# A state-space stage in one block: drive in PSUM, C rows by DMA, two products before two scans

## The chip, the cores and the metric

The kernel runs on one core of one Trainium2 chip. The metric is the device time of one execution in microseconds, lower is better. The core has five engines that run side by side and meet only at semaphores: TensorE (PE; its matmuls write into PSUM), VectorE (DVE), ScalarE (ACT), GpSimd (POOL) and SyncE (SP), which here issues most DMAs.

## The reference

Two decoder layers over 1024 tokens of 128 features, in float32. Layer 0 begins with a Mamba block, then attention to a context of 6404 rows (16 heads, one key and value head), then a mixture of experts; layer 1 has self-attention, attention to the context, and a mixture of experts. After each branch comes a residual sum and a layer norm. The change is in the Mamba block alone, cut here to what matters (256 inner features, 16 states, rank 8):

```
xi, z   = split(x @ W_in.T)                    # 256 features each
xc      = silu(causal_conv4(xi))
dt_r, B, C = split(xc @ W_xproj.T)             # 8, 16 and 16 columns
delta   = softplus(dt_r @ W_dt.T + b_dt)
for each state n of 16, each feature f of 256, along t:
    h[t] = exp(delta[t, f] * A[f, n]) * h[t-1] + delta[t, f] * xc[t, f] * B[t, n]
    y[t, f] += h[t] * C[t, n]
out     = ((y + D * xc) * silu(z)) @ W_out.T
x       = layernorm(x + out)
```

The kernel also makes, in the same stage, the keys and values of layer 0's context attention from the 6404 context rows, since PE and DVE are free for them there. A key is kept as a high half and a low half (float32r).

## The kernel before, in words

Features lie on the partitions (two halves `s` of 128), time (1024) along the free dimension. Each engine's program is written out by hand; its order of instructions is its order of work, and semaphores join the engines.

*Front* (first block, lines 464 to 613). PE makes `xz` (line 517), then value chunks (`keys.values`, line 351: 51 chunks of 128 context rows, each a float32 matmul of 8 columns in two passes), key ranges (`keys.keys`, line 341: 13 ranges of 512 columns), `dbc` (dt_r, B and C, line 531) and the step sizes (line 540: 8 rows contracted). ScalarE or DVE writes a range's high half (lines 362, 371), DVE its low half (line 380). DVE makes the convolution, copies `dbc` from PSUM (line 598), splits it in three bfloat16 parts (`split`, lines 399 to 403), and SyncE moves their B and C rows into `bc_rows` (line 488), whose tile GpSimd has filled with zeros (line 510). Six 1024-wide DVE instructions make `delta` and `u` = delta * xc (lines 611 to 613).

*States* (second block, lines 615 to 733, loops over the 16 states `n`). All tiles are 128 x 1024 and there is one of each:

- PE spreads row B[n] over 128 partitions into `b_all` (PSUM; `spread`, line 624, bfloat16 with 128 rows contracted), and C[n] into `c_ps`. One `b_all` serves both halves.
- ScalarE makes `decay` (line 649) and copies C to SBUF (line 654).
- DVE makes the drive, `drive[s] = b_all * u[s]`, for both halves, PSUM times SBUF into SBUF (line 661), then the two scans `state[s]` = scan(decay[s], drive[s]), both from SBUF (line 667).
- GpSimd makes the read product `read[s] = state[s] * C`, both from SBUF (line 676).
- PE adds `read[s]` to `y[s]` in PSUM with an identity matmul (`add_read`, line 640; four passes of 512 columns for one half).

The order on PE is: y addition of half 0 of state n-1, B of n+1, y addition of half 1, C of n+1. A scan of state n may overwrite `state[s]` when GpSimd has read it, and a read product may overwrite `read[s]` when PE has added it.

*Tail.* DVE gates (y * silu(z), line 723), PE makes the output (line 703), and `residual_norm` (line 142) follows in a block of its own; its first instruction is line 166. After it the context attention begins.

Of the kernel before, what the change touches and what calls it, by code (L numbers as in the profile page):

```python
# [16 lines left out]
F32 = mybir.dt.float32  # L17
# [124 lines left out]
def residual_norm(k, tag, branch, added=False, store=None):  # L142
# [5 lines left out]
    with ExitStack() as tmp:  # L148
# [6 lines left out]
        turned = k.ps(tag + "_turned", [P, T], tmp)  # L155
# [128 lines left out]
class ContextKeys:  # L284

    CUT = 26
    RANGES = [(c0, min(HALF, CTX - c0)) for c0 in range(0, CTX, HALF)]

    def __init__(self, k, banks):
        self.k = k
        self.banks = banks
        self.v_ps = banks[:, HALF:HALF + NCH * HD].rearrange("p (c e) -> p c e", e=HD)
# [3 lines left out]
        self.v_ready = k.sem("ctx_v_ready")  # L298
# [5 lines left out]
    def bank(self, r):  # L304

        b = (4, 5, 6, 7, 0, 4, 5, 6, 7, 2, 3, 0, 2)[r]
        return self.banks[0:SPAN2, b * HALF:(b + 1) * HALF]

    def replicate(self, pool, w_kv):
# [10 lines left out]
        ins.then_inc(self.rep_ready, 1)  # L320
        pool.wait_ge(k.q_w_loaded, 16)
# [7 lines left out]
    def keys(self, pe, ranges, after=None):  # L329

        nc, k = self.k.nc, self.k
        for r in ranges:
            c0, n = self.RANGES[r]
            if r == 0:
                pe.wait_ge(self.ctx_loaded[0], 16)
                pe.wait_ge(self.rep_ready, 1)
            if c0 <= self.CUT * P < c0 + n:
                pe.wait_ge(self.ctx_loaded[1], 16)
            if r >= 5:
                pe.wait_ge(self.k_done, {5: 1, 6: 2, 7: 3, 8: 4, 9: 5, 10: 5, 11: 5, 12: 10}[r])  # L340
            nc.tensor.matmul(self.bank(r)[:, 0:n], k.wk_rep[:], k.ctx_T[:, c0:c0 + n], start=True,
                             stop=True).then_inc(self.k_made, 1)
# [13 lines left out]
    def high_on_act(self, act, ranges):  # L356

        nc, k = self.k.nc, self.k
        for r in ranges:
            c0, n = self.RANGES[r]  # L360
            act.wait_ge(self.k_made, r + 1)
            nc.scalar.activation(k.key_stack[:, c0:c0 + n], self.bank(r)[:, 0:n], ACT.Identity,
                                 bias=k.shift_one[0:SPAN2, :]).then_inc(self.k_high, 1)

    def high_on_dve(self, dve, ranges):

        nc, k = self.k.nc, self.k
        for r in ranges:
            c0, n = self.RANGES[r]
            dve.wait_ge(self.k_made, r + 1)  # L370
            nc.vector.tensor_scalar(k.key_stack[:, c0:c0 + n], self.bank(r)[:, 0:n], k.shift_one[0:SPAN2, :], None,
                                    ALU.add).then_inc(self.k_high, 1)

    def halves(self, dve, ranges):

        nc, k = self.k.nc, self.k
        for r in ranges:
            c0, n = self.RANGES[r]
            dve.wait_ge(self.k_high, r + 1)
            nc.vector.scalar_tensor_tensor(out=k.key_stack[:, c0:c0 + n], in0=k.key_stack[:, c0:c0 + n].bitcast(F32),  # L380
                                           scalar=k.half_sel[0:SPAN2, :], in1=self.bank(r)[:, 0:n], op0=ALU.mult,
                                           op1=ALU.add).then_inc(self.k_done, 1)
# [7 lines left out]
    def take_values(self, dve):  # L390
# [3 lines left out]
        nc.vector.tensor_copy(k.val_ones[0:TAIL, full, 0:HD], self.v_ps[0:TAIL, full, :])  # L394
# [11 lines left out]
def mamba(k):  # L406
# [4 lines left out]
    LOADS = 6  # L411
    ctx = ExitStack()
    with ctx:
# [13 lines left out]
        conv = k.key1_T[:, 2 * T:4 * T].rearrange("p (s t) -> p s t", s=2)  # L427
        xc = k.sb("xc", [P, 2, T], F32, ctx)
        delta = k.sb("delta", [P, 2, T], F32, ctx)
        u = k.sb("u", [P, 2, T], F32, ctx)  # L430
        dbc = k.key1_T[0:ROWS, CTX - T:]

        bc_rows = k.sb("bc_rows", [P, NS, T], BF16, ctx)
        pick = k.sb("bc_pick", [P, 2, P], BF16, ctx)
        early = k.val1[:].rearrange("p c e -> p (c e)")
        decay = early[:, 0:2 * T].rearrange("p (s t) -> p s t", s=2)
        c_all = early[:, 2 * T:4 * T].rearrange("p (s t) -> p s t", s=2)
        state = early[:, 4 * T:6 * T].rearrange("p (s t) -> p s t", s=2)
        dbc_part = [state[0:ROWS, i // 2, (i % 2) * HALF:(i % 2 + 1) * HALF].bitcast(BF16) for i in range(3)]
        dbc_rest = [decay[0:ROWS, i, :] for i in range(2)]  # L440

        read = xpad[:, :, 0:T]
        soft = drive = conv
# [6 lines left out]
        dbc_split, dlt_ready, log_ready = k.sem("dbc_split"), k.sem("dlt_ready"), k.sem("log_ready")  # L450
        act_step, a_exp = k.sem("mamba_act_step"), k.sem("a_exp")
        rows_moved, pick_set, rows_zeroed = k.sem("rows_moved"), k.sem("pick_set"), k.sem("bc_rows_zeroed")
        b_ready, c_ready, b_used, c_copied = k.sem("b_ready"), k.sem("c_ready"), k.sem("b_used"), k.sem("c_copied")
        decay_ready, read_ready, y_added = k.sem("decay_ready"), k.sem("read_ready"), k.sem("y_added")
        scanned = k.sem("scanned")
        gated, out_ready = k.sem("y_gated"), k.sem("mamba_out_ready")


        with ExitStack() as front:
# [1806 lines left out]
```

## Time and profile before

| | us |
|---|---|
| median of 3 runs | 2270.96 (2268.21 to 2271.05) |
| the profiled execution's own time | 2268.48 |
| its span, first to last instruction | 2266.8 |
| granted PE clock, mean over the span | 0.957 of full speed |
| PE busy | 2078.7 (92% of the span) |
| DVE busy | 1625.9 (72%) |
| ACT busy | 1332.4 (59%) |
| POOL busy | 163.8 (7%) |

The busy times are sums over the whole span, and stages with different limits stand in them side by side: the state-space stage is its first tenth, and GpSimd works nearly only there. A granted clock of 1.00 is 2.4 GHz, 0.50 is 1.2 GHz; a value between them for a stretch is a mean of the two. In a timeline row the first number is the start, the second the time that the instruction (or a merged run of them, x2 and more) took; the bracket is the idle time of the engine before it and what ended it. Line numbers are those of the kernel before. A name such as `sb_key_T` or `sb_val` may stand for another tile that lies in the same memory (drive and zs in `key1_T`, decay, C and state in `val1`).

### The profile page before, as it was taken

How to read it: one execution, taken by the hardware profiler on the slowest of the kernel's cores; microseconds unless marked ns; L12 is line 12 of the kernel's file. 1: busy time of each engine (PE TensorE's matmuls, PEld its weight loads, DVE VectorE, ACT ScalarE, POOL GpSimd, SP SyncE). 2: the span in 40 equal slices, each digit the busy share in tenths (PEclk: the TensorE clock that was granted, in tenths of full speed). 3: DMA queues.
4: the chain of work that ended last, by engine and by line, in shares of the span. 5: the costliest groups of instructions: out<-in, count | busy, mean ns of one | idle time of the engine just before them, and what ended most of it. 6: DMA issues, size and time to landing. Idle time of an engine off the chain costs nothing. (4 is left out here: it accounts for less than half of the span.)

```text
span 2266.8 us, 38983 instructions
## 1 busy us (share of the span) xinstructions
PE 2078.7 (92%) x15239; PEld 983.5 (43%) x15240; DVE 1625.9 (72%) x2162; ACT 1332.4 (59%) x2203; POOL 163.8 (7%) x161
## 2 busy tenths in 40 slices
PE   8666899999999999999999999899589997999988
PEld 4222353333333333333333333477433333777755
DVE  6997878988889888898888983223778883444345
ACT  4332247777777777777777778623247773333421
POOL 3574000000000000000000000000200010000000
PEclk8898899999999999999999999899879998999989
DMA  3000000000000000000000000011000000000011
GB/s 107 0 0 1 0 1 1 1 1 1 1 1 1 1 1 1 1 1 1 1 1 1 1 1 1 10 33 37 1 1 1 0 0 1 1 1 0 1 33 32
DMA packets 20767, 16.16 MB, mean 7 GB/s; under 512 B 5520, under 2 KB 20016, under 8 KB 20368
## 3 DMA queue, kind: packets, MB, share of 16 engines
q1 hardware_dynamic: 19440, 12.05, 1.9%
q8 instruction: 103, 1.69, 0.3%
q10 hardware_dynamic: 1184, 2.10, 0.2%
q14 instruction: 40, 0.33, 0.0%
HBM read 13.42 MB, written 0.52 MB: 6 GB/s over the span
## 5 line engine op out<-in xcount | busy, mean ns | idle before, releaser
L966 DVE TENSOR_REDUCE sb_max_partial<-ps_max_ps 128x1 f32<-128x1024 f32 (+1 forms) x896 | 958.1, 1107 | 99.2 <-PE ps_max_ps L809 93.6
L957 ACT ACTIVATE sb_probs<-ps_score_ps 128x512 f32<-128x512 f32 (+1 forms) x1632 | 885.5, 595 | 238.3 <-PE ps_score_ps L929 193.8
L809 PE MATMUL ps_max_ps<-sb_key_stack,sb_q_stack 64*128 64x512 f32 (+1 forms) x1664 | 602.0, 438 | 22.6 <-DVE sb_max_partial L966 10.3
L929 PE MATMUL ps_score_ps<-sb_q_stack,sb_key_stack 64*128 64x512 f32 x1632 | 592.1, 442 | 1.9 <-issue 0.4
L910 PE MATMUL ps_acc_ps<-sb_probs,sb_val_ones 128*32 128x256 f32 x6528 | 521.4, 391 | 0.8 <-ACT sb_probs L957 0.4
L929 PEld LDWEIGHTS ps_score_ps<-sb_q_stack,sb_key_stack 64*128 64x128 f32 x1632 | 241.1, 185 | 280.9 <-ACT sb_probs L957 266.3
L809 PEld LDWEIGHTS ps_max_ps<-sb_key_stack,sb_q_stack 64*128 64x128 f32 x1664 | 252.2, 185 | 152.9 <-DVE sb_max_partial L966 128.4
L910 PEld LDWEIGHTS ps_acc_ps<-sb_probs,sb_val_ones 128*32 128x32 f32 x6528 | 128.4, 108 | 293.6 <-ACT sb_probs L957 218.2
L1661 DVE TENSOR_REDUCE sb_s_max_partial<-ps_s_max_ps 128x1 f32<-128x512 f32 x256 | 170.2, 691 | 42.2 <-PE ps_s_max_ps L1586 35.2
L1651 ACT ACTIVATE sb_s_probs<-ps_s_score_ps 128x1024 f32<-128x1024 f32 x128 | 131.0, 1024 | 49.1 <-PE ps_s_score_ps L1623 46.7
L640 PE MATMUL ps_y<-sb_xpad,sb_ident 128*128 128x512 f32 x128 | 75.5, 721 | 51.6 <-POOL sb_xpad L676 51.6
L1878 DVE TENSOR_SCALAR_CACHE_REDUCE sb_x_scores<-ps_x_score_ps 128x1024 f32<-128x1024 f32 (+1 forms) x56 | 62.1, 1111 | 83.2 <-PE ps_x_score_ps L1819 83.2
L1819 PE MATMUL ps_x_score_ps<-sb_key_T,sb_x_q_buf 128*128 128x512 f32 (+1 forms) x208 | 102.1, 594 | 8.8 <-DVE sb_x_q_buf L1887 8.8
L1846 PE MATMUL ps_x_acc_ps<-sb_val,sb_x_turned 128*128 128x128 f32 (+1 forms) x816 | 109.1, 277 | 1.2 <-DVE sb_x_turned L1858 0.9
L1586 PE MATMUL ps_s_max_ps<-sb_s_k_stack_T,sb_s_q_stack_T 128*128 (+1 forms) x256 | 104.0, 408 | 6.3 <-PEq L1439 2.8
L676 POOL TENSOR_TENSOR sb_xpad<-sb_val 128x1024 f32<-128x1024 f32 x32 | 103.7, 3260 | 64.9 <-DVE sb_val L667 64.9
L1858 ACT COPY sb_x_turned<-ps_x_turn_ps 128x512 f32<-128x512 f32 (+1 forms) x52 | 29.6, 569 | 132.0 <-PE ps_x_turn_ps L1834 132.0
L667 DVE TENSOR_TENSOR_SCAN sb_val<-sb_val,sb_key_T 128x1024 f32<-128x1024 f32 x32 | 102.0, 3227 | 0.6
L1442 POOL MEMSET sb_s_mask<- 128x128 f32 x1 | 0.2, 204 | 1397.8 <-POOLq L160 1397.8
L1846 PEld LDWEIGHTS ps_x_acc_ps<-sb_val,sb_x_turned 128*128 128x128 f32 (+1 forms) x816 | 99.5, 191 | 3.5 <-issue 1.0
L1236 DVE SCALAR_TENSOR_TENSOR sb_e_acc<-ps_e_out_ps,sb_e_gates,sb_e_acc 128x128 f32<-128x128 f32 x136 | 36.7, 344 | 79.7 <-PE ps_e_out_ps L1216 79.7
L649 ACT ACTIVATE sb_val<-sb_delta,sb_a_neg 128x1024 f32<-128x1024 f32 x32 | 36.6, 1148 | 80.8 <-DVE sb_val L667 80.8
(285 smaller groups left out, 1791.8 us busy)
## 6 DMA issues: line engine op xcount, KB each, us to landing
sb_e_w<-L_ffn_rW SPq DMA_DIRECT2D x30, 128.0 KB, 2.1
sb_e_w<-L_ffn_W_T SPq DMA_DIRECT2D x24, 128.0 KB, 2.1
sb_ctx_T<-ctx_T SPq DMA_DIRECT2D x1, 1664.0 KB, 8.1
sb_ctx_T<-ctx_T ACTq DMA_DIRECT2D x1, 1538.0 KB, 9.4
sb_x_T<-x_T SPq DMA_DIRECT2D x1, 512.0 KB, 3.7
sb_x_tok<-x ACTq DMA_DIRECT2D x1, 512.0 KB, 11.6
sb_e_w<-L_ffn_sW SPq DMA_DIRECT2D x4, 128.0 KB, 2.2
out<-sb_x_tok SPq DMA_DIRECT2D x2, 256.0 KB, 2.4
```

Of the source, the lines that this page charges most:

```text
L667: nc.vector.tensor_tensor_scan(state[:, s, :], decay[:, s, :], drive[:, s, :], 0.0, ALU.mult, ALU.add).then_inc(scanned, 1)
L676: nc.gpsimd.tensor_tensor(read[:, s, :], state[:, s, :], c_all[:, parity, :], ALU.mult).then_inc(read_ready, 1)
L809: ins = nc.tensor.matmul(max_ps[:, u % 2, a:a + n], q_stack[rows(blk), blk // 2, h * P:(h + 1) * P], k.key_stack[rows(blk), c0 + a:c0 + a ...
L910: ins = nc.tensor.matmul(acc_ps[32 * q:32 * q + 32, 0:QUART], k.val_ones[:, v, :], probs[:, v % 3, q * QUART:(q + 1) * QUART], start=(v == ...
L929: nc.tensor.matmul(score_ps[:, e % 3, :], k.key_stack[rows(blk), c * P:(c + 1) * P], q_stack[rows(blk), blk // 2, j * HALF:(j + 1) * HALF] ...
L957: nc.scalar.activation(probs[0:n, c % 3, j * HALF:(j + 1) * HALF], score_ps[0:n, e % 3, :], ACT.Exp).then_inc(exp_done, 1)
L966: nc.vector.tensor_reduce(partial[:, h, r:r + 1], max_ps[:, u % 2, 0:RANGES[r][1]], AX.X, ALU.max).then_inc(unit_used, 1)
L1586: nc.tensor.matmul(max_ps[:, u % 2, :].rearrange("p (t c) -> p t c", t=4), block_of(q_T, h, u // 2), half_of(k_T, h, u % 2), start=True, s ...
L1651: nc.scalar.activation(probs[:, c % 2, :], score_ps[:, c % 2, :], ACT.Exp).then_inc(exp_done, 1)
L1661: nc.vector.tensor_reduce(partial[:, u // 2, u % 2:u % 2 + 1], max_ps[:, u % 2, :], AX.X, ALU.max).then_inc(unit_used, 1)
L1819: ins = nc.tensor.matmul(score_ps[:, local % 2, (g % 2) * HALF:(g % 2) * HALF + n], q_buf[:, s, :], k.key1_T[:, g * HALF:g * HALF + n], st ...
L1846: ins = nc.tensor.matmul(acc_ps[:, s, 0:D], turned[0:keys, local % 2, j * P:(j + 1) * P], k.val1[0:keys, c0 + j, :], start=(c0 + j == 0), ...
```

## The change

All in the state-space stage:

- One block instead of two, and unrolled loops instead of loops with a register. PSUM is one tile of eight banks from start to end.
- B and `dbc`: two float32r halves instead of three bfloat16 parts. ScalarE copies the high half, DVE subtracts. Four DMAs bring the B rows to two partitions for each of two groups of states; there is no tile of zeros. A spread is now two float32r matmuls that contract 2 rows, into `drive[s]`: each half has its own spread, and B[n+1] of half s waits for the scan of half s of state n.
- C: stored to DRAM once, and each state's row is loaded by SyncE, replicated over the 128 partitions, with three buffers. The C matmul and ScalarE's copy are gone.
- DVE multiplies the drive in place in PSUM, both halves first, then scans both; the scan reads decay from SBUF and drive from PSUM.
- PE's order per state and half: B of the next state, then the y addition.
- The last read product (state 15, half 1) is DVE's instead of GpSimd's.
- Key ranges 8 to 12 are made after the last state instead of before the first, and the value chunks 12 to 50 in one go ahead of the first state. The step-size matmuls of the two halves have key range 5 and 6 between and behind them.
- The gate writes to `read`, and the norm's transposes use the banks of y.

```diff
+                for i, made in ((0, dbc_high), (1, dbc_low)):
+                    sp.wait_ge(made, 1)
+                    for g in range(GROUPS):
+                        first = DR + g * SLOTS
+                        sp.dma_start(b_rows[32 * g + i:32 * g + i + 1, :, :].bitcast(F32), dbc_half[i][first:first + SLOTS, :].bitcast(F32)).then_inc(b_moved, 16)
...
+        def spread(pe, n, s):
+
+            lo = 32 * (n // SLOTS)
+            if n > 0:
+                pe.wait_ge(scanned, 2 * (n - 1) + s + 1)
+            for h in range(2):
+                ins = nc.tensor.matmul(half(drive[s], h), ones[lo:lo + 2, :], b_rows[lo:lo + 2, n % SLOTS, h * HALF:(h + 1) * HALF],
+                                       start=True, stop=True)
+            ins.then_inc(b_ready, 1)
...
+        def load_c(sp, n):
+
+            if n >= DEPTH:
+                sp.wait_ge(read_ready, 2 * (n - DEPTH) + 2)
+            sp.dma_start(c_all[:, n % DEPTH, :], c_dram[n:n + 1, :].to_broadcast([P, T])).then_inc(c_loaded[n % DEPTH], 16)
...
+            def _(pool):
...
+                for n in range(NS):
+                    c_is_loaded(pool, n)
+                    for s in range(2):
+                        if n == NS - 1 and s == 1:
+                            break
+                        pool.wait_ge(scanned, 2 * n + s + 1)
+                        if n > 0:
+                            pool.wait_ge(y_added, 2 * (n - 1) + s + 1)
+                        nc.gpsimd.tensor_tensor(read[:, s, :], state[:, s, :], c_all[:, n % DEPTH, :], ALU.mult).then_inc(read_ready, 1)
...
+            def _(pe):
...
+                keys.make(pe, 4)
+                pe.wait_ge(keys.k_done, 4)
+                pe.wait_ge(dbc_copied, 1)
+                for s in range(2):
+                    for h in range(2):
+                        ins = nc.tensor.matmul(half(xz[2 + s], h), w_dt[:, s * P:(s + 1) * P], dbc[0:DR, h * HALF:(h + 1) * HALF],
+                                               start=True, stop=True)
+                    ins.then_inc(dlt_ready, 1)
+                    if s == 0:
+                        pe.wait_ge(dbc_low, 1)
+                    keys.make(pe, 5 + s)
+                keys.make(pe, 7)
+                keys.values(pe, w_kv, range(12, NCH))
+
+                pe.wait_ge(keys.rep_ready, 2)
+                pe.wait_ge(b_moved, 16 * 2 * GROUPS)
+                pe.wait_ge(keys.v_taken, 1)
+                pe.wait_ge(keys.k_done, keys.LATE)
+                spread(pe, 0, 0)
+                spread(pe, 0, 1)
...
+                for n in range(NS):
                     for s in range(2):
+                        if n + 1 < NS:
+                            spread(pe, n + 1, s)
+                        elif s == 0:
+                            pe.wait_ge(scanned, 2 * n + 1)
+                            for r in range(keys.LATE, keys.LATE + 2):
+                                keys.make(pe, r)
+                        add_read(pe, n, s)
+                        if n == NS - 1 and s == 0:
+                            keys.make(pe, keys.LATE + 2)
+                for r in range(keys.LATE + 3, len(keys.RANGES)):
+                    keys.make(pe, r)
...
+                for n in range(NS):
                     for s in range(2):
+                        if n == 0:
+                            dve.wait_ge(log_ready, s + 1)
+                            dve.wait_ge(keys.k_done, keys.LATE)
+                            nc.vector.tensor_tensor(delta[:, s, :], delta[:, s, :], soft[:, s, :], ALU.add).then_inc(delta_ready, 1)
+                            dve.wait_ge(delta_ready, s + 1)
+                            link(nc.vector.tensor_tensor(u[:, s, :], delta[:, s, :], xc[:, s, :], ALU.mult))
+                        dve.wait_ge(b_ready, 2 * n + s + 1)
+                        nc.vector.tensor_tensor(drive[s], drive[s], u[:, s, :], ALU.mult).then_inc(driven, 1)
                     for s in range(2):
+                        dve.wait_ge(driven, 2 * n + s + 1)
+                        dve.wait_ge(decay_ready, 2 * n + s + 1)
+                        if n > 0:
+                            dve.wait_ge(read_ready, 2 * (n - 1) + s + 1)
+                        nc.vector.tensor_tensor_scan(state[:, s, :], decay[:, s, :], drive[s], 0.0, ALU.mult, ALU.add).then_inc(scanned, 1)
+                dve.wait_ge(scanned, 2 * NS)
+                c_is_loaded(dve, NS - 1)
+                dve.wait_ge(y_added, 2 * (NS - 1))
+                nc.vector.tensor_tensor(read[:, 1, :], state[:, 1, :], c_all[:, (NS - 1) % DEPTH, :], ALU.mult).then_inc(last_read, 1)
+                for r in range(keys.LATE, keys.LATE + 3):
+                    keys.halve(dve, r)
                 for s in range(2):
+                    dve.wait_ge(y_added, 2 * NS - 1 + s)
+                    nc.vector.tensor_tensor(read[:, s, :], y[s], zs[:, s, :], ALU.mult).then_inc(gated, 1)
+                for r in range(keys.LATE + 3, len(keys.RANGES)):
+                    keys.halve(dve, r)
```

## Rows read from the trace of the kernel before

**Rows 1.** The page: busy tenths of PE in 40 slices of the span
```profile
PE   8666899999999999999999999899589997999988
```

**Rows 2.** Timeline of the state loop: start us, duration us, engine, line, operation
```profile
68.47 4.18 POOL L676 TENSOR_TENSOR sb_xpad<-sb_val 128x1024 f32<-128x1024 f32 x1 [30.23 <-DVE sb_val L667]
71.62 1.22 DVE L661 TENSOR_TENSOR sb_key_T<-ps_b_all,sb_u 128x1024 f32<-128x1024 f32 x1
72.62 2.34 POOL L676 TENSOR_TENSOR sb_xpad<-sb_val 128x1024 f32<-128x1024 f32 x1
72.78 4.33 DVE L667 TENSOR_TENSOR_SCAN sb_val<-sb_val,sb_key_T 128x1024 f32<-128x1024 f32 x1
77.24 4.21 POOL L676 TENSOR_TENSOR sb_xpad<-sb_val 128x1024 f32<-128x1024 f32 x1 [2.29 <-DVE sb_val L667]
86.07 4.17 POOL L676 TENSOR_TENSOR sb_xpad<-sb_val 128x1024 f32<-128x1024 f32 x1 [2.32 <-DVE sb_val L667]
```

**Rows 3.** Three lines of the loop: ns min/median/max, first to last start
```profile
L661 DVE TENSOR_TENSOR sb_key_T<-ps_b_all,sb_u x32: 1191/1206/1225, 63.8 to 194.6; 128x1024 f32<-128x1024 f32 x32
L667 DVE TENSOR_TENSOR_SCAN sb_val<-sb_val,sb_key_T x32: 2257/2274/4328, 66.0 to 200.1; 128x1024 f32<-128x1024 f32 x32
L676 POOL TENSOR_TENSOR sb_xpad<-sb_val x32: 2335/3254/4205, 68.5 to 204.5; 128x1024 f32<-128x1024 f32 x32
```

**Rows 4.** Timeline of the front
```profile
10.55 1.01 ACT L555 COPY sb_xpad<-ps_front_ps 128x1024 f32<-128x1024 f32 x1 [1.44 <-PE ps_front_ps L517]
25.93 1.22 DVE L598 COPY sb_key_T<-ps_front_ps 40x1024 f32<-40x1024 f32 x1 [0.45 <-PE ps_front_ps L531]
27.77 4.11 DVE L380 SCALAR_TENSOR_TENSOR sb_key_stack<-sb_key_stack,sb_half_sel,ps_front_ps 128x512 fp32r<-128x512 f32 x5 [0.63 <-ACT sb_key_stack L362]
30.21 3.19 PE L351 MATMUL ps_front_ps<-sb_w_kv,sb_ctx_T 128*128 128x8 f32 x28
31.80 6.97 DVE L399 CAST sb_val<-sb_key_T 40x1024 bf16<-40x1024 f32 x1
54.36 0.57 DVE L393 COPY sb_val_ones<-ps_front_ps 128x400 f32<-128x400 f32 x1
61.18 1.22 DVE L613 TENSOR_TENSOR sb_u<-sb_delta,sb_xc 128x1024 f32<-128x1024 f32 x1
```

**Rows 5.** Stretches of the front: busy us by engine, granted clock, DMA
```profile
30.00:33.30 3.30, 3.30 (x29) 3.08 (x27) 3.08 (x4) 2.44 (x4) 3.30 (x1) 1.00 0.02 5
36.00:39.50 3.50, 3.50 (x5) 1.00 (x3) 3.47 (x2) 1.11 (x1) 2.23 (x1) 0.50 0.00 0
48.70:52.20 3.50, 3.50 (x19) 3.43 (x19) 0.00 (x0) 0.00 (x0) 0.00 (x0) 0.50 0.00 0
```

**Rows 6.** Timeline of PE in the state loop
```profile
63.51 1.06 PE L624 MATMUL ps_c_all<-sb_bc_rows,sb_bc_pick 128*128 128x512 bf16 x2
90.29 1.98 PE L640 MATMUL ps_y<-sb_xpad,sb_ident 128*128 128x512 f32 x4 [2.53 <-POOL sb_xpad L676]
92.11 0.59 PE L624 MATMUL ps_b_all<-sb_bc_rows,sb_bc_pick 128*128 x2
99.08 3.61 PE L640 MATMUL ps_y<-sb_xpad,sb_ident 128*128 128x512 f32 x4 [4.06 <-POOL sb_xpad L676]
```

**Rows 7.** Stretches of 8.79 us, one a state: first and last of 14
```profile
77.09:85.88 8.79, 4.72 (x10) 1.74 (x9) 8.75 (x6) 3.19 (x3) 6.50 (x2) 0.81 0.00 0
...
191.36:200.15 8.79, 5.87 (x14) 1.93 (x12) 8.75 (x6) 3.19 (x3) 6.48 (x2) 1.00 0.00 1
```

**Rows 8.** Timeline of the tail
```profile
204.55 5.40 PE L640 MATMUL ps_y<-sb_xpad,sb_ident 128*128 128x512 f32 x8 [4.48 <-POOL sb_xpad L676]
211.27 3.84 PE L703 MATMUL ps_b_all<-sb_w_out_T,sb_val 128*128 128x128 f32 x32 [1.32 <-DVE sb_val L723]
215.43 1.42 DVE L166 TENSOR_TENSOR sb_norm_res<-ps_b_all,sb_x_tok 128x512 f32<-128x512 f32 x2 [4.22 <-PEq L678]
```

**Rows 9.** The page: a DMA, its size, us from issue to landing
```profile
sb_x_tok<-x ACTq DMA_DIRECT2D x1, 512.0 KB, 11.6
```

More of the change, by code:

```diff
@@ L327, in replicate, with make @@
                                         float(HD) ** -0.5, None, ALU.mult)
-    def keys(self, pe, ranges, after=None):
+    def make(self, pe, r):
         nc, k = self.k.nc, self.k
[L332 to L342, printed above, removed]
+        c0, n = self.RANGES[r]
+        if r == 0:
+            pe.wait_ge(self.ctx_loaded[0], 16)
+            pe.wait_ge(self.rep_ready, 1)
+        if c0 <= self.CUT * P < c0 + n:
+            pe.wait_ge(self.ctx_loaded[1], 16)
+        if r in self.AFTER:
+            pe.wait_ge(self.k_done, self.AFTER[r])
+        nc.tensor.matmul(self.bank(r), k.wk_rep[:], k.ctx_T[:, c0:c0 + n], start=True, stop=True).then_inc(self.k_made, 1)
     def values(self, pe, w_kv, chunks):
@@ L354, in values, with high_on_act, high_on_dve, halve @@
             ins.then_inc(self.v_ready, 1)
[L356 to L382, printed above, removed]
+    def high_on_act(self, act, r):
+        act.wait_ge(self.k_made, r + 1)
+        self.k.nc.scalar.activation(self.columns(r), self.bank(r), ACT.Identity, bias=self.k.shift_one[:]).then_inc(self.k_high, 1)
+    def high_on_dve(self, dve, r):
+        dve.wait_ge(self.k_made, r + 1)
+        self.k.nc.vector.tensor_scalar(self.columns(r), self.bank(r), self.k.shift_one[:], None, ALU.add).then_inc(self.k_high, 1)
+    def halve(self, dve, r):
+        dve.wait_ge(self.k_high, r + 1)
+        self.k.nc.vector.scalar_tensor_tensor(out=self.columns(r), in0=self.columns(r).bitcast(F32), scalar=self.k.half_sel[:],
+                                              in1=self.bank(r), op0=ALU.mult, op1=ALU.add).then_inc(self.k_done, 1)
     def prepare(self, dve, link):
@@ L427, in mamba @@
         conv = k.key1_T[:, 2 * T:4 * T].rearrange("p (s t) -> p s t", s=2)
+        dbc = k.key1_T[0:ROWS, 4 * T:5 * T]
         xc = k.sb("xc", [P, 2, T], F32, ctx)
@@ L732, in mamba, with wide, half @@
-        residual_norm(k, "norm0", out_ps)
+        banks = k.ps("mamba_ps", [P, 8, HALF], ctx)
+        keys = ContextKeys(k, banks)
+        def wide(b):
+            return banks[:, b:b + 2, :].rearrange("p b t -> p (b t)")
+        xz = [wide(2 * c) for c in range(4)]
+        drive = [wide(0), wide(2)]
+        y = [wide(4), wide(6)]
+        out_ps = wide(2).rearrange("p (t e) -> p t e", t=NT)
+        def half(x, h):
+            return x[:, h * HALF:(h + 1) * HALF]
+        def spread(pe, n, s):
[6 more added lines that the diff above has]
+            ins.then_inc(b_ready, 1)
@@ new lines, in add_read @@
+        def add_read(pe, n, s):
+            if n == NS - 1 and s == 1:
+                pe.wait_ge(last_read, 1)
+            else:
+                pe.wait_ge(read_ready, 2 * n + s + 1)
+            for h in range(2):
+                ins = nc.tensor.matmul(half(y[s], h), k.ident[:], read[:, s, h * HALF:(h + 1) * HALF], start=False, stop=True,
+                                       skip_group_check=True)
+            ins.then_inc(y_added, 1)
+        def load_c(sp, n):
+            if n >= DEPTH:
+                sp.wait_ge(read_ready, 2 * (n - DEPTH) + 2)
+            sp.dma_start(c_all[:, n % DEPTH, :], c_dram[n:n + 1, :].to_broadcast([P, T])).then_inc(c_loaded[n % DEPTH], 16)
@@ L735, in stack_queries @@
+        residual_norm(k, "norm0", out_ps, turned=wide(4))
 def stack_queries(nc, link, whole, part, rest, stack, parts):
```

425 lines of the change are left out of this document (169 added, 256 removed).

## The prediction, before the changed kernel ran

> **What bounds the kernel now.** I read the page's slices first [rows 1]: the change lies in the first tenth of the span (slices 1 to 4), and the rest, where the TensorE (PE) is busy nine tenths of each slice, is the same code. So only the time from the start to the first instruction of `norm0`, which is at 215.43 us [rows 8], can move. It has three pieces: the front, up to the first scan at 66.0 [rows 3]; fifteen steps from one state's first scan to the next one's; and a tail.
>
> Then the durations by line and the single instructions of the state loop, VectorE (DVE) beside GpSimd (POOL). The 32 scans take 2257 to 4328 ns, the 32 read products 2335 to 4205 [rows 3]: each has two lengths. The scan takes 2.27 us, or 4.33 when a read product is under way at its start (72.78); the read product takes 2.34 (72.62), or 4.18 when it is issued just behind a scan (68.47) [rows 2]. They take turns: one state is two scans and two reads at about 2.2 each, and their sum is the distance of two states, 8.8 us (77.24 to 86.07, GpSimd's starts [rows 2]); from the second scan that starts at 77.11 to the one at 200.1 [rows 3] they are fourteen times 8.79. The drive product isn't in that sum: at 71.62 it runs inside the time in which read and scan take turns and takes its 1.22 us, and over all 32 its durations are 1191 to 1225 ns [rows 3]. It reads one operand from PSUM and one from SBUF; the scan reads two from SBUF. PE does not bound the loop: its y additions, even at half clock, end before anybody needs them.
>
> Fifteen steps are 131.85 us, and the last state's first scan ends where its second starts, at 200.1 [rows 3]; from there to `norm0` are 15.3 us.
>
> **The front.** Up to the copy of `dbc` at 25.93 [rows 4] nothing on the path changes. Before, what follows on the path is the three-part split, whose first cast took 6.97 us for 40 rows (a plain copy of the same size took 1.22) beside a GpSimd fill, late key ranges, and the last of six 1024-wide DVE instructions, at 61.18 to 62.4 [rows 4]. The change drops cast, fill and five of thirteen key ranges (they go to the tail). What is left, in order: copy ends 27.15. PE's step-size matmuls (8 passes of 512 columns, 8 rows) come in two halves, each followed by key matmuls: at full clock 0.43 a pass, so 27.2 to 28.9 and, after the low half is made (27.15, plus a copy of about 1.05 on ScalarE, bounded by the 1.01 us of a 128-row copy [rows 4], plus 1.22 for the subtraction, as for the copy of the same size), key range 5 at 29.5 to 30.4, second half to 32.1, ranges 6 and 7 to 33.8. Then 38 value chunks, 76 passes: 0.114 us each at full clock (3.19/28), 0.21 at half (about 17 in the 3.5 us from 48.7 to 52.2) [rows 4, 5]. The end is 42.5 with full clock all the way, 53.2 if it is half from 30.4 on (3.4 + 3.4 + 16.0). The stretches of rows 5 show how such work fares: PE was 100% busy from 30.00 to 33.30 with 8-column value passes at full clock, and 100% busy from 36.00 to 39.50 with the 8-row step-size passes at a clock of 0.50: it fell and stayed down with no idle time. From 48.7 to 52.2, value passes again, it was at 0.50 too. I take 49.5, nearer the slow end. DVE then takes the values (0.57 [rows 4] and a four-row copy, to 50.4), and makes two deltas, two u and two drive products, 2 x (1.22 + 1.22 + 1.21) = 7.3 and some 0.3 of waits: first scan at 58.0. Against 66.0 that is **-8.0 us** (bounds -15 and -4). ScalarE's table loads and logarithms (to about 39 to 43) lie under the value passes, and so do the B rows' four DMAs and the first C load, issued from about 30 on (the slowest load of 512 KB landed in 11.6 us [rows 9]). If the cover were gone each would cost its lateness against 50.
>
> **The loop.** Now drive comes through PSUM (B spread there, multiplied in place), so the scan reads one operand from SBUF and one from PSUM, as the drive product does [rows 2]. I take that it no longer waits for GpSimd, nor GpSimd for it: scan 2.27, read 2.34. For the scan's operand in PSUM I price nothing, as the drive product with one (1.19 to 1.23) costs what the products without one do (1.22 at 61.18); the far bounds are the two scan durations, 2.26 and 4.33 [rows 3, 4]. The in-place write into PSUM is shown by no row; from the same two rows I take 1.2, between 1.19 and 1.25.
>
> What now waits last is set by the order. PE's queue per state is: spread of the next B for half 0, y addition of half 0, spread for half 1, y addition of half 1. DVE's is: product 0, product 1, scan 0, scan 1. Product 1 needs spread 1, which stands on PE behind y addition 0, which waits for GpSimd's read of scan 0; and behind product 1 stand both scans. From the end of scan 0 of one state: 0.14 until GpSimd starts (72.78 + 4.33 = 77.11 to 77.24 [rows 2]), read 2.34, 0.05 to PE (taken, no row of these shows it alone), y addition 1.82 to the next matmul's start (90.29 to 92.11), spread 0.59 to its end (92.11, two 512-wide matmuls) [rows 6], 0.05, product 1.16 until scan 0 can start, scan 2.27: **8.4 us a state at full clock**. Scan 1 and product 0 (3.4 us) and GpSimd's second read (to 4.8) lie beside it. At half clock the y addition costs 3.45 (3.61 against 1.98 from start to end, so 1.63 more than 1.82) and the spread 1.06 (63.51) [rows 6]: **10.5 us a state**. Full clock would save 15 x 0.39 = 5.9 us, half clock would add 15 x 1.71 = 25.7.
>
> So PE's clock, which hid behind GpSimd, now counts. In the fourteen full states of before, 8 have a granted clock of 0.81 to 0.83 and 6 one of 0.98 or 1.00 [rows 7]; it falls over the gap of 4.06 us between the last C spread and the next y addition (99.08 [rows 6]), and is back in the unbroken burst of 128-row matmuls that follows; a mean of 0.81 is some 3.3 us of the 8.79 at half clock. In the new loop, at full clock, the gap between y additions is 8.4 - 4.1 = 4.4 us and holds only a spread of 2 rows; rows 5 let me take such narrow work for idleness. The burst between is shorter (no C spread) and is split by another 2-row spread, so a clock that has fallen comes back later. I take 11 of 15 states at half clock (between the 8 of 14 of before and all): 15 x 8.4 + 11 x 2.1 = 149.1, against 131.85: **+17.2 us** (bounds -5.9 and +25.7).
>
> **The tail.** From the end of the last scan 0: scan 1 to 2.3; its read product on DVE 1.2, after GpSimd's, to 3.7; low halves of ranges 8 to 10 (0.8 each, five in 4.11 us [rows 4]), the last at 7.1 since its matmul stands behind y addition 0; two gates as long as the products at 61.18 [rows 4], to 9.6; output matmuls 3.84 to 13.6 [rows 8]; 0.3 to `norm0`: 13.9 against 15.3, **-1.4 us**. The five late key ranges lie beside this on PE (4.0 us in all) except for about a microsecond. PE is busy through it; should it start at half clock as before (204.55, eight passes in 5.40 us [rows 8]), up to 7 us are given back: 3.84 once more and 1.6 for each of two y additions.
>
> **Sum.** -8.0 + 17.2 - 1.4 = +7.8 on the profiled execution's 2268.48: **2276 us**. That execution is 2.5 under the median of the runs, 2270.96, and near their lowest; phase of the clock against the loop makes runs of either kernel differ, and I let the sum stand.
>
> **The pages.** Rows 2 and 3 show scans and reads taking turns and drive products untouched. The Trainium skill (SBUF — State Buffer, the list under its diagram) says the same as a rule: a DVE operation with two SBUF inputs and a GpSimd operation that reads SBUF hold a shared port exclusively for a whole instruction. This trace agrees (4.33 against 2.27). By that rule alone, with everything else hidden, the new loop would be bounded by DVE's own 6.8 us a state, 30 us less than before.
> Rows 5 show the clock falling while PE was 100% busy with narrow matmuls. The Trainium skill (TensorE: Matmul & The Clock Gate, part 1) has the gate follow how busy PE has been. By that, narrow matmuls would keep it open in the front and mostly in the loop, and the time would be that of rival A. This trace speaks against it.
>
> **Rivals.**
> A, faster: PE keeps its full clock in the loop. For it: the gap of 2.53 us before 90.29 did not lower it [rows 6], and the new loop is never without any matmul for over 2 us. Against it: rows 5. Then -8.0 - 5.9 - 1.4 = -15.3: 2253; with a full clock in the front too, 2246. Chance 0.15.
> B, few states at half clock, 4 to 7: 8.4 to 14.7 are added to -15.3, so -7 to -1, and no change is in reach (break-even at 7.3 states): 2262 to 2268, up to 2271 with a slower front. 0.12.
> C, all states at half clock: -8.0 + 25.7 - 1.4 = +16.3: 2285. 0.10.
> D, the scan still takes turns with the read, although one operand is in PSUM: scan 1 then goes first and the read ends 2.2 later, 10.6 at full and 12.7 at half clock: +27 to +58 in the loop: 2286 to 2318. Rows 3 speak against it (no drive product of the 32 was stretched). 0.04.
> E, the C rows come late: a 512 KB load took 11.6 us to land [rows 9], and three are in flight, so each has two states, 17 us. A late one costs its lateness. 0.02.
> My forecast, 8 to 13 states at half clock, holds the remaining 0.57: 2268 to 2284.
>
> **The numbers.** What a measurement can tell from no change is 0.2%, here 4.5 us around 2271. Faster: A, and a quarter of B: 0.18. Same: the rest of B and the low end of the forecast (8 or 9 states, with a good front): 0.22. Slower: 0.60. The range leaves out A's lower part and D: 2254 to 2289; the forecast's own is given above.
>
> **What would show it.** First scan at about 58 (54 to 62); the value passes partly at 0.21. No scan over 2.4 us and no read product over 2.5. DVE idle 1.5 to 4 us before each second drive product, ended by PE's spread. Distances of 8.4 or 10.5 us between first scans, nothing between except where the clock changes inside a y addition, and a granted clock of about 0.65 over the loop. From the last scan 0's end to `norm0` 14 us. I am wrong if scans still show 4.3 us (D), if the loop's clock is over 0.9 (A), or if another wait stands before the drive product.

## The result and the profile after

The changed kernel takes 2284.01 us (median of 20 runs, 2278.29 to 2290.72), the kernel before 2271.01 beside it (20 runs, 2262.64 to 2286.25): **a ratio of 1.0043, 95% interval 1.0026 to 1.0061**. It is slower by 13 us, and the interval leaves out 1. The forecast was 2276, slower, within a range of 2254 to 2289. One execution among all of this document, of experiment 7, took 4517.49 us at a granted clock of 0.46; its ratio leaves it out.

The profiled execution of the changed kernel took 2288.68 us. I read it as the prediction cut it, with the end of a state's first scan as the border (that first scan itself, 2.27 us in both, lies between the first two rows of the table):

| piece | before, us | after, us | difference | predicted |
|---|---|---|---|---|
| front, to the start of the first scan | 66.03 | 61.39 | -4.6 | -8.0 |
| loop, fifteen steps | 131.85 | 153.4 | +21.5 | +17.2 |
| tail, last first scan's end to `norm0` | 15.3 | 13.4 | -1.9 | -1.4 |
| `norm0` starts at | 215.43 | 230.42 | +15.0 | +7.8 |
| the rest, unchanged code | 2051.4 | 2056.6 | +5.2 | 0 |

The page's slices of PE, in tenths, answer [rows 1]: only the first slices hold other work than before.

```profile
PE   8767799999999999999999999899679997999988
```

The three lines of the loop, as in [rows 3]: count, ns min/median/max, first and last start. No scan and no read product has its second, long duration any more; the drive product writes in place into PSUM at its old price.

```profile
L708 DVE TENSOR_TENSOR ps_mamba_ps<-ps_mamba_ps,sb_u x32: 1206/1232/1233, 56.6 to 213.6; 128x1024 f32<-128x1024 f32 x32
L714 DVE TENSOR_TENSOR_SCAN sb_key_T<-sb_val,ps_mamba_ps x32: 2259/2268/2277, 61.4 to 216.9; 128x1024 f32<-128x1024 f32 x32
L548 POOL TENSOR_TENSOR sb_xpad<-sb_key_T,sb_val x31: 2336/2352/2362, 63.8 to 217.2; 128x1024 f32<-128x1024 f32 x31
```

One state in the timeline (answers [rows 2, 6]; start, duration, engine, line, operation, count, and in the bracket the idle time before it with what ended it). L472 is the spread of B, L483 the y addition:

```profile
102.13 4.45 DVE L714 TENSOR_TENSOR_SCAN sb_key_T<-sb_val,ps_mamba_ps 128x1024 f32<-128x1024 f32 x2
...
104.46 0.73 PE L472 MATMUL ps_mamba_ps<-sb_b_rows,sb_b_ones 2*128 2x512 f32 x2 [1.59 <-DVE sb_key_T L714]
104.54 4.66 POOL L548 TENSOR_TENSOR sb_xpad<-sb_key_T,sb_val 128x1024 f32<-128x1024 f32 x2 [5.56 <-DVE sb_key_T L714]
106.50 1.21 DVE L708 TENSOR_TENSOR ps_mamba_ps<-ps_mamba_ps,sb_u 128x1024 f32<-128x1024 f32 x1
...
106.94 3.58 PE L483 MATMUL ps_mamba_ps<-sb_xpad,sb_ident 128*128 128x512 f32 x4 [1.76 <-POOL sb_xpad L548]
...
110.45 0.73 PE L472 MATMUL ps_mamba_ps<-sb_b_rows,sb_b_ones 2*128 2x512 f32 x2
...
111.11 1.99 PE L483 MATMUL ps_mamba_ps<-sb_xpad,sb_ident 128*128 128x512 f32 x4
111.22 1.23 DVE L708 TENSOR_TENSOR ps_mamba_ps<-ps_mamba_ps,sb_u 128x1024 f32<-128x1024 f32 x1 [3.52 <-PE ps_mamba_ps L472]
...
112.36 2.28 DVE L714 TENSOR_TENSOR_SCAN sb_key_T<-sb_val,ps_mamba_ps 128x1024 f32<-128x1024 f32 x1
```

This is the chain that the prediction named. Scan 0 ends at 104.40 (102.13 + 2.27); GpSimd starts at 104.54, its read takes 2.35, PE starts the y addition at 106.94, and at half clock the next spread comes only 3.51 later, at 110.45. Product 1 starts 0.77 after that, scan 0 of the next state 1.14 later, and it takes 2.27: 0.14 + 2.35 + 0.05 + 3.51 + 0.77 + 1.14 + 2.27 = 10.23. DVE is idle 3.52 of it. Over the stage, the waits (total us, times, longest) have this one fifteen times:

```profile
DVE ps_mamba_ps L708 <- PE ps_mamba_ps L472: 52.6, 15, 3.5
```

Three stretches, each a state (answers [rows 7]; the columns are the stretch, its length, busy time and count of PE, PE's weight load, DVE, ACT and POOL, then the granted clock and DMA):

```profile
71.52:81.70 10.18, 6.83 (x13) 2.43 (x12) 6.72 (x6) 2.30 (x2) 4.66 (x2) 0.83 0.16 52
...
102.13:112.36 10.23, 6.88 (x13) 2.44 (x12) 6.71 (x5) 2.30 (x2) 4.66 (x2) 0.83 0.16 53
204.51:214.75 10.24, 6.90 (x13) 2.43 (x12) 6.72 (x5) 2.30 (x2) 4.66 (x2) 0.83 0.01 2
```

In [rows 7] states at 0.81 and at 1.00 stood side by side. Here each of the fifteen states has y addition 0 at half clock and the rest at full: the steps are 10.13, 10.18, 10.21 and then 10.23 to 10.25, while y addition 0 grows from 3.46 us in the first to 3.58 in the later ones. A granted clock of 0.83 over 10.24 us is some 3.5 us at half.

The front (answers [rows 4, 5]), first as a timeline, then the value passes as a stretch. All 78 passes ran at half clock, PE busy without a break:

```profile
37.15 16.35 PE L359 MATMUL ps_mamba_ps<-sb_w_kv,sb_ctx_T 128*128 128x8 f32 x78
...
53.53 0.57 DVE L386 COPY sb_val_ones<-ps_mamba_ps 128x400 f32<-128x400 f32 x1 [14.48 <-PE ps_mamba_ps L359]
...
61.39 4.45 DVE L714 TENSOR_TENSOR_SCAN sb_key_T<-sb_val,ps_mamba_ps 128x1024 f32<-128x1024 f32 x2
```

```profile
37.20:53.50 16.30, 16.30 (x79) 16.16 (x77) 1.82 (x3) 3.33 (x4) 0.00 (x0) 0.50 0.04 15
```

The tail (answers [rows 8]): the last read product on DVE, the output matmuls, `norm0`.

```profile
219.24 1.35 DVE L718 TENSOR_TENSOR sb_xpad<-sb_key_T,sb_val 128x1024 f32<-128x1024 f32 x1
...
226.25 3.84 PE L613 MATMUL ps_mamba_ps<-sb_w_out_T,sb_xpad 128*128 128x128 f32 x32 [0.81 <-DVE sb_xpad L723]
230.42 1.42 DVE L166 TENSOR_TENSOR sb_norm_res<-ps_mamba_ps,sb_x_tok 128x512 f32<-128x512 f32 x2 [3.17 <-PEq L496]
```

### The profile page after: what moved, and what is told of

The parts are those of the page before. It is cut to its first block and busy times, and to the rows that moved or that the text cites. A ratio compares the mean times of both kernels' runs of the same rounds, so it can differ in the third digit from the quotient of the medians.

```text
span 2287.0 us, 38636 instructions
## 1 busy us (share of the span) xinstructions
PE 2107.2 (92%) x15240; PEld 998.8 (44%) x15240; DVE 1585.6 (69%) x2158; ACT 1319.5 (58%) x2189; POOL 118.1 (5%) x156
## 5 line engine op out<-in xcount | busy, mean ns | idle before, releaser
L1655 DVE TENSOR_REDUCE sb_s_max_partial<-ps_s_max_ps 128x1 f32<-128x512 f32 x256 | 170.2, 690 | 42.5 <-PE ps_s_max_ps L1580 35.8
L483 PE MATMUL ps_mamba_ps<-sb_xpad,sb_ident 128*128 128x512 f32 x128 | 87.2, 818 | 26.9 <-POOL sb_xpad L548 26.9
L1598 PE MATMUL ps_s_acc_ps<-sb_s_probs,sb_s_v_buf 128*32 128x256 f32 x1024 | 82.2, 393 | 1.4 <-ACT sb_s_probs L1645 1.1
L1219 ACT ACTIVATE sb_e_hidden<-ps_e_hid_ps,sb_e_b 128x1024 f32<-128x1024 f32 x34 | 37.7, 1112 | 78.6 <-PE ps_e_hid_ps L1199 78.6
L548 POOL TENSOR_TENSOR sb_xpad<-sb_key_T,sb_val 128x1024 f32<-128x1024 f32 x31 | 72.3, 2352 | 123.8 <-DVE sb_key_T L714 123.8
```

What stands on the lines that cost most here:

```text
L483: ins = nc.tensor.matmul(half(y[s], h), k.ident[:], read[:, s, h * HALF:(h + 1) * HALF], start=False, stop=True, skip_group_check=True)
L1598: ins = nc.tensor.matmul(acc_ps[32 * j:32 * j + 32, 0:QUART], v_buf[:, s, v, :], probs[:, v % 2, j * QUART:(j + 1) * QUART], start=(v == 0 ...
L1655: nc.vector.tensor_reduce(partial[:, u // 2, u % 2:u % 2 + 1], max_ps[:, u % 2, :], AX.X, ALU.max).then_inc(unit_used, 1)
```

## The experiments

Two things had to be told apart: **the order** (the loop is slow because product 1, and both scans behind it, wait for a spread that stands on PE behind y addition 0) and **the clock** (each such wait is long because PE's clock falls in a loop whose matmuls between y additions are narrow). Beside them stood the claim that moving the drive into PSUM is what freed scans and reads from each other. Times are medians; the ratio is against the kernel before on the same chip (2274.98 for the first four, 2276.6 for the others). The diffs are against the changed kernel. Clocks and steps are each from one profiled execution.

**1. PE's order: both spreads ahead of both y additions.**

```diff
+                    if n + 1 < NS:
+                        spread(pe, n + 1, 0)
+                        spread(pe, n + 1, 1)
                     for s in range(2):
...
-                            spread(pe, n + 1, s)
```

> One edit to the changed kernel: on TensorE both B spreads of the next state come before the two y additions, so the second spread no longer stands behind the first y addition. VectorE keeps its order (two products, then two scans). My theory (the step is read 0, y addition 0, spread 1, product 1, scan 0): the y additions leave the path, product 1 follows product 0 without idle time, and a state takes VectorE's own four instructions, 2 x 1.14 + 2 x 2.2 = 6.7 to 6.9 us against 10.24, so 15 x 3.4 = 51 us less than the changed kernel: about 2233, and about 38 less than before. Rival: VectorE is slow by itself, since its products write PSUM and its scans read it, or since GpSimd still holds it up; then the distance stays over 9 us and the time over 2265.

Measured: 2237.26 us (2227.68 to 2250.57), ratio 0.9813, interval 0.9759 to 0.9868. The timeline of one state:

```profile
126.34 2.34 DVE L711 TENSOR_TENSOR ps_mamba_ps<-ps_mamba_ps,sb_u 128x1024 f32<-128x1024 f32 x2
126.47 0.73 PE L472 MATMUL ps_mamba_ps<-sb_b_rows,sb_b_ones 2*128 2x512 f32 x2 [1.33 <-DVE sb_key_T L717]
127.13 3.96 PE L483 MATMUL ps_mamba_ps<-sb_xpad,sb_ident 128*128 128x512 f32 x8
128.58 4.45 DVE L717 TENSOR_TENSOR_SCAN sb_key_T<-sb_val,ps_mamba_ps 128x1024 f32<-128x1024 f32 x2
```

The two products run as one block (x2), the two scans follow, and DVE has no idle time in any of the four: the step from this state to the next is 6.61. Ten of the fifteen steps are that long. The other five are 6.89 to 6.92: in each of them a product waited for a spread, 0.9 us in all five, because the two y additions ahead of it ran in part at half clock (5.40 us instead of 3.96 in four of the five). The wait was the order's; with it gone the loop is DVE's own work, and by the two ratios (0.9813 and 1.0043) this kernel is 2.3% faster than the changed one, some 52 us.

**2. DVE's order: product, scan, product, scan.** PE's order is as changed.

```diff
                     for s in range(2):
                         ...
                         nc.vector.tensor_tensor(drive[s], drive[s], u[:, s, :], ALU.mult).then_inc(driven, 1)
-                    for s in range(2):
                         dve.wait_ge(driven, 2 * n + s + 1)
```

> One edit to the changed kernel: VectorE does product 0, scan 0, product 1, scan 1 (the order of two products before two scans is undone); TensorE keeps spread 0, y addition 0, spread 1, y addition 1. My theory: product 1 now stands behind scan 0, which gives y addition 0 and spread 1 another 3.3 us of cover; they stay hidden at full clock and just about at half clock: 6.8 to 7.0 us a state, 2233 to 2236. Rival (the order on VectorE costs nothing, the drive in PSUM or the clock does): within 5 us of the changed kernel's 2284.

Measured: 2244.26 (2240.19 to 2252.46), ratio 0.9860 (0.9811 to 0.9909). Spread 1 still stands behind y addition 0, but scan 0 doesn't stand behind product 1:

```profile
110.32 1.21 DVE L708 TENSOR_TENSOR ps_mamba_ps<-ps_mamba_ps,sb_u 128x1024 f32<-128x1024 f32 x1
...
111.56 2.29 DVE L713 TENSOR_TENSOR_SCAN sb_key_T<-sb_val,ps_mamba_ps 128x1024 f32<-128x1024 f32 x1
...
112.94 1.98 PE L483 MATMUL ps_mamba_ps<-sb_xpad,sb_ident 128*128 128x512 f32 x4 [0.84 <-POOL sb_xpad L548]
113.76 1.21 DVE L708 TENSOR_TENSOR ps_mamba_ps<-ps_mamba_ps,sb_u 128x1024 f32<-128x1024 f32 x1
```

The first step was 11.45 us and all others 6.89 or 6.90; so the time is 8 us and more over the expectation, of which the first step makes 4.6. The steps at 6.89 confirm the order by its other half: either queue turned is enough. Products before scans is not bad in itself: with PE's spreads first it is 0.27 us a state quicker than taking turns (6.62).

**3 and 4. The clock, with the order left alone.** Before the first spread of each state four passes of 512 columns go into the drive's banks, which the spread then overwrites; they wait for what the spread waits for. In 3 they contract 128 rows, in 4 two rows.

```diff
+            if n > 0 and s == 0:
+                for h in range(2):
+                    nc.tensor.matmul(half(drive[0], h), k.ident[0:P, :], xc[0:P, 0, h * HALF:(h + 1) * HALF], start=True, stop=True)
```

```diff
+                    nc.tensor.matmul(half(drive[0], h), k.ident[lo:lo + 2, :], xc[lo:lo + 2, 0, h * HALF:(h + 1) * HALF], start=True, stop=True)
```

> Two idle-time matmuls are added to the changed kernel: before each first spread of a state, behind the same wait, TensorE multiplies the identity (128 rows) with xc into drive 0, 4 passes of 512 columns, which the spread then overwrites. They lie in the gap before y addition 0. My theory (the gap between y additions holds nothing but a 2-row spread, and lets the clock fall before y addition 0): the clock stays at 1.00 through the loop, y addition 0 takes 1.8 us to the next start instead of 3.5, and the distance falls from 10.24 to 8.3 to 8.5 us: 27 us less than the changed kernel, about 2257, in spite of more work on TensorE. Rival (the clock has nothing to do with it): unchanged or, with 1.7 us more on TensorE a state, slower than 2284.

> The same as the run with the identity's 128 rows, but the added matmuls contract 2 rows (of the identity and of xc): as many passes, as many columns, the same place, the same busy time of TensorE. It tells apart what keeps the clock up. My theory (narrow work doesn't count for the clock, as in the front): the clock falls as in the changed kernel, a distance of 10.0 to 10.5 us, time within 6 us of 2284. Rival (the clock follows how busy TensorE is, whatever it contracts): the same as with 128 rows, 8.4 us a state and about 2257.

Measured: with 128 rows 2260.39 (2257.96 to 2268.40), ratio 0.9946 (0.9920 to 0.9971); with two rows 2283.64 (2278.52 to 2289.66), ratio 1.0037 (1.0011 to 1.0063). A state of 3 as a stretch and in the timeline, then a state of 4 (columns as above; L473 is the added work, L475 the spread, L486 the y addition):

```profile
104.91:113.63 8.72, 7.13 (x17) 2.62 (x16) 6.83 (x5) 2.30 (x2) 4.69 (x2) 1.00 0.16 56
```

```profile
107.24 1.98 PE L473 MATMUL ps_mamba_ps<-sb_xc,sb_ident 128*128 128x512 f32 x4 [1.59 <-DVE sb_key_T L717]
...
109.15 0.73 PE L475 MATMUL ps_mamba_ps<-sb_b_rows,sb_b_ones 2*128 2x512 f32 x2
109.81 1.98 PE L486 MATMUL ps_mamba_ps<-sb_xpad,sb_ident 128*128 128x512 f32 x4
```

```profile
112.36:122.60 10.24, 8.63 (x17) 3.20 (x18) 6.83 (x5) 2.30 (x2) 4.67 (x2) 0.83 0.09 29
```

```profile
126.07 1.98 PE L473 MATMUL ps_mamba_ps<-sb_xc,sb_ident 2*128 2x512 f32 x4 [1.59 <-DVE sb_key_T L717]
127.49 1.03 PE L475 MATMUL ps_mamba_ps<-sb_b_rows,sb_b_ones 2*128 2x512 f32 x2
128.56 3.57 PE L486 MATMUL ps_mamba_ps<-sb_xpad,sb_ident 128*128 128x512 f32 x4
```

In the two states shown the added passes take 1.98 us, whether of 128 rows or of two, and start 1.59 after PE's last work. With 128 rows the clock was 1.00 in every state and the step 8.72. With two rows it fell in every state. From the sixth state on it fell as in the changed kernel, although PE was busy 8.63 of 10.24 us, and y addition 0 took 3.57. In the first five it fell further (0.59 to 0.78 by state, steps of 9.91 to 12.40), and in four of these PE was busy without a break, as here:

```profile
81.29:91.21 9.92, 9.92 (x17) 3.49 (x17) 6.83 (x6) 2.30 (x2) 4.68 (x2) 0.67 0.15 54
```

So it is the clock that makes 10.24 of 8.72, and what lets it fall here is that the work between the y additions is narrow, not that PE is idle. Fewer rows also mean fewer multiplications; which of the two counts isn't told apart. Kernel 3 does more work than the changed one and is 1.0% faster (ratios 0.9946 and 1.0043). Its 8.72 is also a measurement of what the order alone costs at full clock: 2.1 us a state over experiment 1. That is nearly all that the free scans could save, since the kernel before had 8.79 and experiment 1 has 6.6.

The Trainium skill (TensorE: Matmul & The Clock Gate, part 1) has the gate follow how busy PE has been. [rows 5] did not agree with that, if busy means what the trace shows as busy, and experiment 4 doesn't either (9.92 of 9.92 us busy at a clock of 0.67).

**5. The drive product written to SBUF.** The spread still goes through PSUM; the product writes to the free end of `key1_T`, the scan reads it there. Two waits ahead of the loop make sure that its old content has been moved.

```diff
+                dve.wait_ge(c_stored, 16)
+                dve.wait_ge(b_moved, 16 * 2 * GROUPS)
...
-                        nc.vector.tensor_tensor(drive[s], drive[s], u[:, s, :], ALU.mult).then_inc(driven, 1)
+                        nc.vector.tensor_tensor(drive_sb[:, s, :], drive[s], u[:, s, :], ALU.mult).then_inc(driven, 1)
...
-                        nc.vector.tensor_tensor_scan(state[:, s, :], decay[:, s, :], drive[s], 0.0, ALU.mult, ALU.add).then_inc(scanned, 1)
+                        nc.vector.tensor_tensor_scan(state[:, s, :], decay[:, s, :], drive_sb[:, s, :], 0.0, ALU.mult, ALU.add).then_inc(scanned, 1)
```

> One edit to the changed kernel: the drive product writes its result to SBUF instead of PSUM (B is still spread into PSUM), so the scan again reads two operands from SBUF. Orders and everything else stay. My theory (two SBUF operands on VectorE and GpSimd's read product take turns; a scan with one does not): scan 1 goes first and read 0 ends about 2.1 us later, so read products of 4.2 us come back, and since read 0 is at the head of the path a state takes 12.2 to 12.5 us instead of 10.24: 30 us more than the changed kernel, about 2315. Rival (the place of the drive makes no difference, the turns of before came from something else): scans 2.27, reads 2.35, time within 5 us of 2284.

Measured: 2316.74 (2315.03 to 2320.21), ratio 1.0176 (1.0126 to 1.0227). The two lines:

```profile
L549 POOL TENSOR_TENSOR sb_xpad<-sb_key_T,sb_val x31: 2336/4179/4199, 62.2 to 250.1; 128x1024 f32<-128x1024 f32 x31
```

```profile
L717 DVE TENSOR_TENSOR_SCAN sb_key_T<-sb_val,sb_key_T x32: 2262/2273/2281, 59.7 to 249.8; 128x1024 f32<-128x1024 f32 x32
```

The long duration is back, this time on GpSimd alone: read 0 is issued beside scan 1 and takes 4.18. It stands in the chain, so a step is 12.02 to 12.78 (five of 12.02 to 12.09 at a clock of 0.82 or 0.83, ten of about 12.77 at 0.60 to 0.63), and the kernel is 1.3% slower than the changed one (ratios 1.0176 and 1.0043). The drive in PSUM does free the two engines from each other; it is the part of the change that works.

**6. Both orders turned** (the diffs of 1 and 2 together).

> Both edits of the earlier runs: both spreads first on TensorE, and product, scan, product, scan on VectorE. If the order on VectorE were a fault by itself, this would beat the run with the spreads first alone. My theory: once the spreads are first, two products before two scans are no fault, they even hide the hand-over from product to scan; the step is 6.9 us as in the run with the alternate order, the first scan comes at 55 instead of 61, and the time is 2238 to 2244. Rival: a step below 6.6 us, and a time under 2232.

Measured: 2243.53 (2235.42 to 2250.61), ratio 0.9840 (0.9788 to 0.9893). The first two steps are 11.46 and 7.85, then 6.89 to 6.92 but for one of 8.55. It is experiment 2's loop, not experiment 1's: what DVE pays for taking turns doesn't hang on PE. The two orders are not additive; each removes the same wait.

**7. The front without most value passes.** Value chunks 12 to 48 are left out, so the values of those context rows are missing.

```diff
-                keys.values(pe, w_kv, range(12, NCH))
+                keys.values(pe, w_kv, range(NCH - 2, NCH))
```

> Value chunks 12 to 48 are left out of the front (chunks 49 and 50 stay), so their 74 passes are gone and the values of those context rows are not computed: the run is read for the front alone. My theory (the value passes at half clock are what holds the first scan): TensorE's front ends about 15.7 us earlier, at 38, VectorE's own work ends at about 39, and the first scan comes at 47 to 48 instead of 61.4. The distance between states stays at 10.0 to 10.3 us. Rival (the front is bound by ScalarE's or VectorE's chain or by the B rows' DMAs): the first scan stays beyond 55.

Measured: 2274.54 (seven of 8 runs from 2268.30 to 2277.38), ratio 0.9993 (0.9960 to 1.0027). The timeline has the first scan 14.1 us earlier, with the copy of the values shifted from 53.53 to 39.45:

```profile
37.29 0.41 PE L359 MATMUL ps_mamba_ps<-sb_w_kv,sb_ctx_T 128*128 128x8 f32 x4
...
39.45 0.57 DVE L386 COPY sb_val_ones<-ps_mamba_ps 128x400 f32<-128x400 f32 x1
...
47.30 4.45 DVE L714 TENSOR_TENSOR_SCAN sb_key_T<-sb_val,ps_mamba_ps 128x1024 f32<-128x1024 f32 x2
```

So the value passes do set the end of the front, one for one. The loop, entered at another time, went through steps of 10.93, 9.78 and 8.64 and then stood at 10.24 again; `norm0` starts at 215.21, 15.2 before the changed kernel's. By the two ratios (0.9993 and 1.0043) the whole is 0.5% faster, some 11 us.

**8. The best of it: spreads first, and one wide addition** (the diff of 1, and before the first spread of each state this one matmul):

```diff
+            if n > 0 and s == 0:
+                nc.tensor.matmul(half(drive[0], 0), k.ident[:], xc[:, 0, 0:HALF], start=True, stop=True)
```

> Spreads first on TensorE, and one idle-time matmul (128 rows, 2 passes) before each first spread. With the spreads first the steps were 6.62 us at full clock and 6.9 where the clock fell. My theory: with the fill the clock stays up, all steps are 6.62 to 6.7, 1 to 2 us less than with the spreads first alone, about 2235. Rival: the fill delays the spreads and with them product 0, steps of 6.9 or more.

Measured: 2232.41 (2228.50 to 2239.76), ratio 0.9798 (0.9749 to 0.9846), the fastest of all and faster than both kernels. Against experiment 1, a stretch of each loop, 100 and 101 us long; first experiment 8, then 1:

```profile
60.00:160.00 100.00, 92.80 (x209) 33.56 (x210) 100.00 (x61) 34.51 (x30) 70.25 (x30) 1.00 0.20 69
```

```profile
61.00:162.00 101.00, 83.82 (x177) 31.34 (x176) 100.09 (x62) 34.51 (x30) 70.05 (x30) 0.92 0.19 68
```

DVE is busy all of the 100 us, every step is 6.61 or 6.62, the clock 1.00. Over experiment 1 the intervals overlap, so that the addition is worth anything in the whole time isn't shown. In the profile it takes the steps of 6.9 away, which is 1.5 us. `norm0` starts 5.6 us earlier than in experiment 1 (173.87 against 179.51), but 2.3 of that come from the front and 1.9 from the tail.

## Why the prediction was right in direction and short in size

**The front.** Predicted -8.0, measured -4.6. The step that failed is the value passes: I let them end at 49.5, between the two ends of the sum (42.5 and 53.2), though [rows 5] had shown half clock in such passes; they ended at 53.5, 4.0 later, all at half clock (16.35 us for 78, where I had counted 76; 0.21 each). The slow end of the sum was right to 0.3. What follows them was 7.9 instead of 8.5.

**The scan and the read.** Both at 2.27 and 2.35 as predicted, the in-place product at 1.23 (taken: 1.2). Experiment 5 shows that this is due to the operand in PSUM, and rival D falls with it. The rule of the Trainium skill that the prediction cites (SBUF — State Buffer, the list under its diagram) agrees with both sides of that experiment (read products of 2.35 beside a scan with one SBUF operand, 4.18 behind one with two). That DVE's own work can be the bound, which I worked out beside it as 6.8 us a state, is what experiment 1 measures, at 6.6; the changed kernel's order forbids it.

**The chain of a state.** All its links are there in the order predicted. At full clock it was put at 8.4 and is 8.72 (experiment 3): the float32r spread of two rows takes 0.73 to its end and not the 0.59 of the bf16 spread of [rows 6], and with the four passes ahead the y addition starts 0.14 after the read instead of 0.05, and the next spread 1.91 behind it instead of 1.82. At half clock it was put at 10.5 and is 10.24, since the clock is back when spread 1 runs (0.73 and not 1.06).

**How many states.** I took 11 of 15 at half clock; all fifteen were. That is the term that was mis-sized. By my own lengths, all fifteen would have made 157.5 where 11 made 149.1; the half-clock state was 0.26 shorter than I had it, which gives back some 4, and 153.4 was read. To `norm0` the sum was 7.2 short: 4.3 in the loop, 3.4 in the front, less 0.5 in the tail. The reason for a mixture was [rows 7], where 8 of 14 states were slow: there GpSimd and DVE set the step of 8.79 whatever the clock did, and the clock fell in about every second state. In the new loop the fall is in the chain; the step lengthens by it, and stays at 10.24, where each state meets it in the same place. The steps of experiment 7, which leave 10.93 and 8.64 and come to rest at 10.24 too, show the same; why it comes to rest just there isn't settled. My forecast of 0.65 for the loop's clock was wrong too, it was 0.83: some 3.5 us of each state at half are enough to hold y addition 0 entirely.

**The tail.** -1.9 against -1.4; the clock was full in the output matmuls (3.84).

**Rivals.** Rival C (all states at half clock, 2285) is what happened, and I had given it 0.10; at 2284.01 the time is its, not that of the middle of my forecast. That it fits to 1 us is in part luck: its front was 3.4 too quick and its loop 4.2 too slow. My wide range held the time only because it reached from A's to C's. Rival A is what experiment 3 makes of the kernel: 2260 measured, 2253 forecast. Its loop was to save 5.9 and takes 130.8 against 131.85. E did not occur: no drive product and no read waits for a C row.

**The rest.** The same code after `norm0` took 5.2 us more in the profiled execution. The medians show no such loss: they differ by 13.0 in all, and the traces by 15.0 up to `norm0`.

## What to carry to other kernels

When work is moved off the path, write down the in-order queue of each engine around it: here a spread of 0.7 us on PE stood behind a y addition that waits for GpSimd, and on DVE two scans stood behind the product that needs that spread, which cost nearly all that was saved at full clock (8.72 a state against 8.79 before) and more than that at half (10.24), while turning either queue made the kernel 1.4 to 1.9% faster than before. A TensorE that was off the path may have run at half clock unseen; before it is put on the path, read its clock in stretches, and don't count on narrow matmuls to keep it up: here neither passes of two rows nor passes of 8 columns did. Don't carry over the share of passes in which it fell, either: it fell in 8 of 14 states while it was off the chain, and in 15 of 15 once it was in it.

## What was not expected of the hardware

- Two rows or 128, a pass of 512 columns takes the same time, yet only the wide ones kept the clock at 1.00 (experiments 3 and 4: 8.72 against 10.24 a state). 8-column passes with 128 rows, back to back for 16.3 us, ran at 0.50 throughout, where in the kernel before such passes ran 3.19 us at 1.00 behind wide ones ([rows 4, 5]).
- The loop settles at 10.24 us a state with the clock at 0.50 for about a third of it, from different starts (changed kernel, experiment 4 after five states, experiment 7 after three).
- DVE is quicker with two products and then two scans (6.62 a state) than taking turns (6.89), though in stretches of the loop it is busy 99% of the time or more either way (experiment 8: all of 100 us; experiment 2: 95.1 of 96). Why isn't shown.
- The code after `norm0` is the same in all ten kernels (before, changed, eight experiments), yet took 2049.9 to 2069.4 us in their profiled executions, one each; the stretches of it at clock 0.50 came to 130.0 us in the one and 181.2 in the other (before: 2051.4 with 133.5). Longest and shortest go with most and nearly least time at half clock; no experiment changed that time alone, so it is a correlation. Since a gain of 14 us in the front (experiment 7) is of the size of this spread, the span of one profiled execution can't price such a change, but the time of the piece that it touches can.
